# Prologue of a graph kernel: the first visit's tiles pass both convolutions ahead of the others, gather and copy back by visits

## The chip, the cores and the metric

The kernel runs on one core of one Trainium2 chip. The metric is the device time of one execution in microseconds; lower is better. Of the core's engines the text names TensorE (PE in the profile; PEld is its weight load), VectorE (DVE), ScalarE (ACT), GpSimd (POOL) and SyncE (SP), which here only issues DMAs. Each engine works through its own list of instructions in order; semaphores hold one engine until another has got somewhere.

## The reference

The input `x` is 64 graphs of 128 nodes with 128 features, `adj` 64 matrices of 128 x 128. Two stages follow each other, each with a residual and a layer norm over the features:

```
def gcn(x, adj):                          # on the first 25 nodes of each graph only
    for g, idx in enumerate(GROUPS):      # 25, 9, 7, 6, 6 nodes
        A = normalise(adj[:, idx][:, :, idx] + eye)
        h   = relu(A @ (x[:, idx] @ W1[g]) + b1[g])       # 128 -> 256
        out = relu(A @ (h @ W2[g]) + b2[g])               # 256 -> 128
        fused[:, idx] += softmax(fusion_w)[g] * out
x = layernorm(x + gcn(x, adj))
A = (adj != 0)
h = x
for l in range(5):
    h = gru(A^T @ (h @ weight[l]), h)     # one GRU cell, shared weights
out = layernorm(x + h * mask)
```

## The kernel before

All is written out by hand: five lists of instructions, one for each engine, with counters that one engine waits on and another raises. No planner orders anything; what stands first in the program of an engine runs first.

The 64 graphs are sixteen **visits** of four graphs each, and four **chunks** of sixteen graphs (four visits). The GRU layers run in 80 windows, four visits in turn; window k multiplies one visit's state by the gate weights (TensorE), applies the gates (ScalarE, VectorE) and forms the difference `dg` (GpSimd). The first stage of chunk c + 1 is spread over windows of chunk c. Only chunk 0 has nothing to hide behind: it is computed in the **prologue**, and this is what the change touches.

In the prologue the group of 25 nodes is four tiles (`TA`) of four graphs each, 100 rows; tile t is just visit t. The small groups are five tiles (`TB`): group 1 in two tiles of eight graphs, groups 2, 3 and 4 in one tile each of sixteen. For both halves the order is: adjacency transposed and scaled (`na`, `nb`), product with the node rows `xt` (`neighbours`, into `ya`, `yb`), W1 and ReLU (`hidden_a`, `hidden_b`), W2 (`second_a`, `second_b1`, `second_b2`, into `s2`), product with `na` or `nb` (`output_a`, `output_b`). ScalarE writes group 0 into `fused` and the small groups into `part`; VectorE adds `part` into `fused` with five adds (`gather`). Then TensorE multiplies the GRU's input weights for layers 2 to 4 (`fused_weights`), transposes `fused` back for all four visits (`back_visit`, waits for all five adds) and runs filler: 18 transposes of the identity (`stay_warm`) and 12 products with no reader.

For each visit VectorE adds the transposed rows into `xn` (`add_visit`) and takes the statistics (`norm1`); GpSimd makes the reciprocal root with a power (`deviation1`); the normalisation is shared, two graphs on ScalarE and two on GpSimd, for visit 0 on VectorE instead of GpSimd (`half_norm1`). Then TensorE transposes the visit into the GRU's layout (`enter`, lines 1247 and the waits ahead of it) and the windows begin. GpSimd also turns `an` into the 0/1 mask for visits 2 and 3 (`ones`), VectorE for visits 0 and 1. The lists that matter here, of VectorE and of GpSimd:

```
gather(0); ones(0); add_visit(0); norm1(0); add_visit(1); norm1(1)
half_norm1(0, HALVES[1]); add_visit(2); add_visit(3); lo_state(0, PL)
...
ones(2); deviation1(0); deviation1(1); norm1(1)
ones(3); deviation1(2); norm1(2); power(1)
```

Of the kernel before, what the change touches and what calls it, by code (L numbers as in the profile page):

```python
# [7 lines left out]
NG = len(GROUPS)  # L8
# [121 lines left out]
def build(nc, x, adj, nodemask, W1, b1, W2, b2, fusion_w, weight, w_ih, w_hh, b_ih, b_hh, out):  # L130
# [3 lines left out]
    with ctx:  # L134
# [5 lines left out]
        def sem(name):  # L140
# [77 lines left out]
        ALONE = dict(adj=(P[0], P[2]), y=(P[5], P[4]), ha=(P[0], P[2]), hb=(P[5], P[3]), s=(P[4], P[1], P[0]),  # L218
                     o=(P[2], P[5]))

# [6 lines left out]
        def b1c(g, c):  # L227
            return biasc[:, g * HC + c:g * HC + c + 1]
# [22 lines left out]
            "bn1", "ln1_st", "ln1_rs", "ln1_ok", "sum_ok", "bn2", "ln2_st", "ln2_rs", "ln2_ok", "out_ok"))  # L251
        gathered, dev1, dev2, ln1_dve, ln1_pool, hT_ok, ln2_dve = map(sem, (
# [64 lines left out]
        ADDS = 5  # L317

# [53 lines left out]
        def _(pool):  # L372
# [97 lines left out]
            ones(2)  # L470
# [3 lines left out]
            ones(3)  # L474
            deviation1(2)
            norm1(2)
            power(1)
# [35 lines left out]
        def _(act):  # L513
# [38 lines left out]
            def hidden_b1(c):  # L552

                act.wait_ge(h_ps, 4 * c + 4)
# [67 lines left out]
            neighbours(0)  # L622
# [107 lines left out]
        def _(dve):  # L730
# [75 lines left out]
            def neighbours(c):  # L806

                dve.wait_ge(y_ps, 2 * c + 2)
                nc.vector.tensor_copy(yb[:], banks(c)["y"][1][:, 0:COLS_B]).then_inc(yb_ok, 1)

            def hidden_b0(c):

                dve.wait_ge(h_ps, 4 * c + 3)
                for g in range(1, NG):
                    a, b = group_cols(g)
                    last = TS(hb[:, 0, a:b], banks(c)["hb"][0][:, a:b], b1c(g, 0), 0.0, ALU.add, ALU.max)
                last.then_inc(hb0_ok, 1)

            def second_b1(c):

                dve.wait_ge(s_ps, 3 * c + 2)
                nc.vector.tensor_copy(s2[0:ROWS[4], 4:6, :], banks(c)["s"][1][0:ROWS[4], 0:256].rearrange("p (t d) -> p t d", t=2)).then_inc(sb_ok, 1)

            def second_b2(c):

                dve.wait_ge(s_ps, 3 * c + 3)
# [4 lines left out]
            def gather(c):  # L831

                dve.wait_ge(oa_ok, c + 1)
                for g, done, (into, these) in gather_parts():
                    dve.wait_ge(ob_ok, (NG - 1) * c + g)
                    if done:
                        dve.wait_ge(gathered, ADDS * c + done)
                    TT(into, into, these, ALU.add).then_inc(gathered, 1)
# [213 lines left out]
        def _(pe):  # L1052
# [61 lines left out]

            def hidden_a(c):
# [87 lines left out]
            stay_warm(8, P[5])  # L1203
# [3 lines left out]
            TR(P[3][:, GATES:512], wl[:, 4, :], ident[:]).then_inc(prep_t, 1)  # L1207
            pe.wait_ge(wit_ok, 1)
# [9 lines left out]
            neighbours(0)  # L1218
# [3 lines left out]
            pe.wait_ge(w1_in, 16)  # L1222
            hidden_a(0)
            pe.wait_ge(prep_a, 1)
            hidden_b(0)
            pe.wait_ge(w2_in, 16)
            second_a(0)
            pe.wait_ge(prep_lo, 3)
            second_b1(0)
            second_b2(0)  # L1230
            output_a(0)
            output_b(0)
            pe.wait_ge(mask_in, 16)
            TR(P[3][:, GATES:GATES + B], maskr[:], ident[0:B, 0:B])
            fused_weights(2)
            fused_weights(3)
            fused_weights(4)
            pe.wait_ge(gathered, ADDS)
            for visit in range(SLOTS):
                back_visit(visit)  # L1240
            stay_warm(18, PG)
            for _ in range(12):
                MM(PG[:, 0:128], wh[:, 0, 0:128], wh[:, 0, 128:256], start=True, stop=True)
# [162 lines left out]
```

## Time and profile before

| | |
|---|---|
| median of 3 runs | 534.74 us (534.69 to 535.28) |
| the profiled execution | 534.39 us |
| its span, first to last instruction | 532.1 us |
| TensorE busy | 514.9 us (97%) |
| VectorE, ScalarE, GpSimd busy | 437.5, 369.4, 249.3 us |

A row of the timeline merges instructions of one line that follow each other; its first number is when the first starts, its second how long all of them take. Matmul ends are modelled and overlap the next start, so several matmuls in a row go out faster than their lengths add up to. An fp32 matmul is two matmul instructions ("passes"), a transpose one. The idle time in square brackets is that of the engine just before the row, with what ended it. Spans on GpSimd are rough.

### The profile page before, as it was taken

The numbers are of one execution on the slowest core, as the hardware profiler recorded it, in microseconds if no ns is written. First come the engines' busy times: TensorE is split into PE (matmuls) and PEld (weight loads), VectorE is DVE, ScalarE is ACT, GpSimd is POOL, SyncE is SP. The second block draws the span as 40 slices with busy tenths as digits, with TensorE's granted clock in tenths as the row PEclk, the third lists the DMA queues.
The fourth block names the chain that finished last, engine by engine and source line by source line (L and its number), as shares of the span: only waits on it lengthen the run. The fifth ranks groups of instructions, "written<-read, shape, count | busy, mean of one in ns | idle before, by whom it ended". The sixth has DMA issues, their size and how long they took to land.

```text
span 532.1 us, 8535 instructions
## 1 busy us (share of the span) xinstructions
PE 514.9 (97%) x2993; PEld 441.2 (83%) x2993; DVE 437.5 (82%) x970; ACT 369.4 (69%) x683; POOL 249.3 (47%) x299
## 2 busy tenths in 40 slices
PE   7999999999999999999999999999999999999991
PEld 6888889888888889888888889888888888888870
DVE  5479775899979877889979986688988998877886
ACT  2468665767876676787786676787785678786645
POOL 7569422458532354457633254546552245332334
PEclk9999999999999999999999999999999999999995
DMA  5967610000000000000000000000000000010002
GB/s 138 220 181 178 165 34 4 1 1 0 2 1 0 9 25 22 21 20 22 1 1 1 1 0 22 22 20 21 0 2 1 1 1 20 25 37 0 1 0 79
DMA packets 35579, 17.29 MB, mean 32 GB/s; under 512 B 4321, under 2 KB 35498, under 8 KB 35538
## 3 DMA queue, kind: packets, MB, share of 16 engines
q1 hardware_dynamic: 32233, 14.99, 10.7%
q10 hardware_dynamic: 2665, 1.54, 1.0%
q8 instruction: 24, 0.39, 0.3%
q0 software_dynamic: 640, 0.22, 0.3%
q14 instruction: 17, 0.14, 0.1%
HBM read 12.54 MB, written 4.19 MB: 31 GB/s over the span
## 4 chain that ended last, share of the span: by engine, by line
PE 92%; DVE 3%; SPq 2%; DMA 1%; ACT 1%; POOL 1%; issue 0%; DVEq 0%; POOLq 0%
PE p L1260 20%; PE p L1262 20%; PE p L1261 20%; PE p L1254 13%; PE p L1247 8%; PE p L1138 3%; PE p L1112 1%; PE p L1131 1%; PE p L1121 1%; DMA xt<-in_x_dram 1%; SPq L273 1%; PE p L1176 1%; SPq L268 1%; PE p L1168 1%; DVE st L930 0%; PE p L1063 0%
## 5 line engine op out<-in xcount | busy, mean ns | idle before, releaser
L486 POOL TENSOR_TENSOR dg<-hT,ng 128x512 f32<-128x512 f32 x80 | 126.1, 1576 | 255.7 <-ACT ng L706 255.6
L1260 PE MATMUL p<-ghi,wf 128*128 128x512 f32 x240 | 101.1, 421 | 0.0
L1260 PE MATMUL p<-hhi,wh 128*128 128x512 f32 x237 | 99.6, 420 | 0.0
L1262 PE MATMUL p<-ghi,wf 128*128 128x512 f32 x240 | 94.4, 393 | 0.0
L1261 PE MATMUL p<-glo,wf 128*128 128x512 f32 x240 | 93.6, 390 | 0.0
L1262 PE MATMUL p<-hhi,wh 128*128 128x512 f32 x237 | 93.1, 393 | 0.0
L1261 PE MATMUL p<-hlo,wh 128*128 128x512 f32 x237 | 92.5, 390 | 0.0
L1010 DVE SCALAR_TENSOR_TENSOR cg<-p,biasc,rg 128x512 f32<-128x512 f32 x80 | 59.9, 748 | 37.8 <-ACT rg L688 36.8
L688 ACT ACTIVATE rg<-p,gb 128x512 f32<-128x512 f32 x80 | 55.4, 692 | 34.8 <-PE p L1262 29.0
L706 ACT ACTIVATE ng<-cg,biasc 128x512 f32<-128x512 f32 x80 | 57.9, 724 | 23.1 <-DVE cg L1013 22.7
L1254 PEld LDWEIGHTS p<-an,nat 128*128 128x128 f32 x512 | 66.9, 191 | 5.1
L702 ACT ACTIVATE zg<-p,gb 128x512 f32<-128x512 f32 x80 | 55.1, 688 | 18.0 <-PE p L1262 17.8
L1254 PE MATMUL p<-an,nat 128*128 128x128 f32 x512 | 67.3, 274 | 0.0
L901 DVE TENSOR_TENSOR hlo<-hT,hhi 128x512 fp32r<-128x512 f32 x76 | 66.2, 871 | 0.8
L1013 DVE TENSOR_TENSOR cg<-cg,p 128x512 f32<-128x512 f32 x80 | 55.1, 688 | 8.7 <-DVE cg L1010 0.5
L907 DVE TENSOR_TENSOR glo<-p,ghi 128x512 fp32r<-128x512 f32 x80 | 55.1, 690 | 5.5 <-ACT ghi L653 5.5
L915 DVE TENSOR_TENSOR hT<-ng,dg 128x512 f32<-128x512 f32 x80 | 55.5, 694 | 2.8
L913 DVE TENSOR_TENSOR dg<-zg,dg 128x512 f32<-128x512 f32 x80 | 55.1, 689 | 0.0
L1247 PE MATMUL p<-ident,hT 128*128 128x128 f32 x320 | 49.1, 276 | 5.4 <-DVE hT L915 5.3
L1262 PEld LDWEIGHTS p<-ghi,wf 128*128 128x128 f32 x240 | 45.0, 188 | 10.4
L684 ACT COPY nat<-p 128x512 f32<-128x512 f32 x64 | 37.7, 589 | 22.6 <-PE p L1247 21.9
L1262 PEld LDWEIGHTS p<-hhi,wh 128*128 128x128 f32 x237 | 44.5, 188 | 9.9
(157 smaller groups left out, 846.9 us busy)
## 6 DMA issues: line engine op xcount, KB each, us to landing
xn<-in_x_dram SPq DMA_DIRECT2D x8, 512.0 KB, 4.8
an<-in_adj_dram SPq DMA_DIRECT2D x8, 512.0 KB, 7.4
out_dram<-xn SPq DMA_DIRECT2D x15, 256.0 KB, 2.3
xt<-in_x_dram SPq DMA_DIRECT2D x16, 50.0 KB
w<-in_L_gnn_W_dram ACTq DMA_DIRECT2D x1, 640.0 KB, 5.8
w<-in_L_gnn_W_dram SPq DMA_DIRECT2D x1, 640.0 KB, 4.4
zg<-in_L_gnn_weight_dram ACTq DMA_DIRECT2D x1, 320.0 KB, 3.9
xt<-in_x_dram SPq DMA_DIRECT2D x8, 36.0 KB
```

The source lines that it names most:

```text
L486: nc.gpsimd.tensor_tensor(dg[:, w.k % 2, :], hT[:, w.slot, :], ng[:, w.k % 2, :], ALU.subtract).then_inc(d_ok, 1)
L688: nc.scalar.activation(rg[:, p, :], PR[:], ACT.Sigmoid, bias=gb[:, 0:1]).then_inc(r_ok, 1)
L702: nc.scalar.activation(zg[:, p, :], PZ[:], ACT.Sigmoid, bias=gb[:, 1:2]).then_inc(z_ok, 1)
L706: nc.scalar.activation(ng[:, p, :], cg[:, p, :], ACT.Tanh, bias=bin_).then_inc(n_ok, 1)
L901: TT(hlo[:, m % SLOTS, :], hT[:, m % SLOTS, :] if source is None else source[:], hhi[:, m % SLOTS, :], ALU.subtract).then_inc(lo_ok, 1)
L915: TT(hT[:, s, :], ng[:, p, :], dg[:, p, :], ALU.add).then_inc(h_ok, 1)
L1010: STT(cg[:, p, :], PH[:], bhn, rg[:, p, :], ALU.add, ALU.mult).then_inc(t1_ok, 1)
L1247: last = TR(bank[:, q * 128:(q + 1) * 128], src(q), ident[:])
L1254: last = MM(bank[:, q * N:(q + 1) * N], src(q), an[:, b + q, :], start=True, stop=True)
L1260: MM(bank[:], w[:, 0, cols], xhi, start=start, stop=False)
L1261: MM(bank[:], w[:, 0, cols], xlo, start=False, stop=False)
L1262: return MM(bank[:], w[:, 1, cols], xhi, start=False, stop=stop)
```

## The change

Only the prologue of chunk 0 changes; no arithmetic is dropped.

- TensorE's `neighbours(0)` becomes `first_neighbours`: tile 0 of group 0, then the five small-group tiles, then tiles 1 to 3. `first_chunk` replaces the steps from `hidden_a` to `output_b`: tile 0 passes W1 first, then the small groups, then tiles 1 to 3 as one block of 300 columns; W2 and the output likewise, tile 0 ahead, tile 1 before the small groups' output, tiles 2 and 3 after it. Tile 0 has banks of its own (`TILE0`).
- ScalarE copies and activates tile 0 apart from tiles 1 to 3; the activation of the small groups' output is split by visits: four small ones for visit 0, five for the others. VectorE copies `s2` of tiles 1 to 3 (`s1_ok`), which ScalarE did before.
- The gather is split: five adds for visit 0, five for visit 1, five for visits 2 and 3 (`gather_visits`), on VectorE. `back_visit(0)` waits for the first five only; then the three `fused_weights`, then `back_visit(1)`, `(2)`, `(3)`.
- GpSimd's `ones(2)` moves behind the second visit's half, `ones(3)` behind the third's.
- Filler: 8 becomes 14 and 7 are added early on; 18 becomes 8 and 12 becomes 8 at the end.

```diff
@@ places of the banks
+        TILE0 = dict(y=P[6], h=P[7], s=P[6], o=P[7])
+        LATER = slice(ROWS[0], COLS_A)
@@ GpSimd
-            ones(2)
             deviation1(0)
             deviation1(1)
             norm1(1)
-            ones(3)
+            ones(2)
             deviation1(2)
             norm1(2)
+            ones(3)
             power(1)
@@ ScalarE, prologue
-            neighbours(0)
+            act.wait_ge(y0_ps, 1)
+            nc.scalar.copy(ya[:, 0:ROWS[0]], TILE0["y"][:, 0:ROWS[0]]).then_inc(ya0_ok, 1)
+            act.wait_ge(y_ps, 2)
+            nc.scalar.copy(ya[:, LATER], ALONE["y"][0][:, LATER]).then_inc(ya_ok, 1)
             ...
-            hidden_a(0)
+            act.wait_ge(h0_ps, 1)
+            for h in range(HC):
+                nc.scalar.activation(ha[:, h, 0:ROWS[0]], ..., bias=b1c(0, h)).then_inc(ha0_ok, 1)
             hidden_b1(0)
-            second_a(0)
+            for h in range(HC):
+                act.wait_ge(h_ps, 3 + h)
+                nc.scalar.activation(ha[:, h, LATER], ALONE["ha"][h][:, LATER], ACT.Relu, bias=b1c(0, h)).then_inc(ha_ok, 1)
+            act.wait_ge(s0_ps, 1)
+            nc.scalar.copy(s2[0:ROWS[0], 0, :], TILE0["s"][0:ROWS[0], 0:D]).then_inc(sa_ok, 1)
             act.wait_ge(b_ok, 1)
-            output_a(0)
-            output_b(0)
+            act.wait_ge(o0_ps, 1)
+            nc.scalar.activation(by_rows[:, 0, :, 0:FN], TILE0["o"][:, 0:ROWS[0]]...).then_inc(oa0_ok, 1)
+            act.wait_ge(o_ps, 1)
+            for g in range(1, NG):
+                first_part(g, 0, SB).then_inc(ob0_ok, 1)
+            first_part(1, SB, SB)
+            first_part(1, 2 * SB, 2 * SB).then_inc(ob_ok, 1)
+            for g in range(2, NG):
+                first_part(g, SB, 3 * SB).then_inc(ob_ok, 1)
+            act.wait_ge(o_ps, 2)
+            nc.scalar.activation(by_rows[:, 1:, :, 0:FN], ALONE["o"][0][:, LATER]...).then_inc(oa_ok, 1)
             high_weights(2)
@@ VectorE, prologue
             second_b1(0)
             second_b2(0)
-            gather(0)
+            dve.wait_ge(s_ps, 3)
+            nc.vector.tensor_copy(s2[0:ROWS[0], 1:4, :], ALONE["s"][0][0:ROWS[0], D:4 * D]...).then_inc(s1_ok, 1)
+            gather_visits(0, SB, oa0_ok, ob0_ok, visit0_ok)
             ones(0)
             add_visit(0)
             norm1(0)
+            gather_visits(SB, SB, oa_ok, ob_ok, visit1_ok)
+            gather_visits(2 * SB, 2 * SB, oa_ok, ob_ok, gathered)
             add_visit(1)
@@ TensorE, the new middle
+                second(0, TILE0["s"], 0).then_inc(s0_ps, 1)
+                pe.wait_ge(prep_lo, 3)
+                second_b1(0)
+                second_b2(0)
+                pe.wait_ge(sa_ok, 1)
+                MM(TILE0["o"][:, 0:ROWS[0]], s2[0:ROWS[0], 0, :], na[0:ROWS[0], 0:ROWS[0]],
+                   start=True, stop=True).then_inc(o0_ps, 1)
+                pe.wait_ge(ha_ok, HC)
+                second(1, ALONE["s"][0], D)
+                output_b(0)
+                second(2, ALONE["s"][0], 2 * D)
+                second(3, ALONE["s"][0], 3 * D).then_inc(s_ps, 1)
+                ...
+                pe.wait_ge(s1_ok, 1)
+                for t in TA[1:]:
+                    ...
+                last.then_inc(o_ps, 1)
```

TensorE from the end of the outputs to the first entering transposes (line 1247 before, 1364 after; `p4<-ident,fused` is the first visit's way back, `p6<-ng,cg` the fused weights of layer 2). Before:

```order
L1234 MATMUL p3<-ident,maskr 128x64
L1057 MATMUL p6<-ng,cg 128x384
L1057 MATMUL p0<-ng,cg 128x384
L1057 MATMUL p3<-ng,cg 128x384
L1195 MATMUL p4<-ident,fused 25x128 x4
L1195 MATMUL p1<-ident,fused 25x128 x4
L1195 MATMUL p7<-ident,fused 25x128 x4
L1195 MATMUL p2<-ident,fused 25x128 x4
L1189 MATMUL p5<-ident 128x128 x18
L1243 MATMUL p5<-wh 128x128 x12
L1247 MATMUL p6<-ident,xn 128x128 x4
```

And after:

```order
L1233 MATMUL p3<-ident,maskr 128x64
L1237 MATMUL p2<-na,s2 128x100 x3
L1320 MATMUL p4<-ident,fused 25x128 x4
L1120 MATMUL p6<-ng,cg 128x384
L1120 MATMUL p0<-ng,cg 128x384
L1120 MATMUL p3<-ng,cg 128x384
L1320 MATMUL p1<-ident,fused 25x128 x4
L1320 MATMUL p7<-ident,fused 25x128 x4
L1320 MATMUL p2<-ident,fused 25x128 x4
L1314 MATMUL p5<-ident 128x128 x8
L1360 MATMUL p5<-wh 128x128 x8
L1364 MATMUL p6<-ident,xn 128x128 x4
```

The first visit's transposes now stand ahead of the three weights, behind the output of tiles 1 to 3 (line 1237); the other visits' stand behind the weights.

VectorE from the first visit's add into `xn` to its half of the normalisation (line 895 before, 953 after). Before:

```order
L845 TENSOR_TENSOR xn<-xn,p4 25x512
L871 BN_STATS st1<-xn 128x6 x4
L875 BN_AGGR ag1<-st1 128x2 x4
L845 TENSOR_TENSOR xn<-xn,p1 25x512
L871 BN_STATS st1<-xn 128x6 x4
L875 BN_AGGR ag1<-st1 128x2 x4
L895 TENSOR_SCALAR xn<-xn,rs1,nm1 128x128 x2
```

And after, from the ten adds that follow the first visit's statistics:

```order
L896 TENSOR_TENSOR fused<-fused,part 128x4x9
L896 TENSOR_TENSOR fused<-fused,part 128x4x6
L896 TENSOR_TENSOR fused<-fused,part 128x4
L896 TENSOR_TENSOR fused<-fused,part 128x2x3x4 x2
L896 TENSOR_TENSOR fused<-fused,part 128x8x9
L896 TENSOR_TENSOR fused<-fused,part 128x8x6
L896 TENSOR_TENSOR fused<-fused,part 128x8
L896 TENSOR_TENSOR fused<-fused,part 128x2x3x8 x2
L903 TENSOR_TENSOR xn<-xn,p1 25x512
L929 BN_STATS st1<-xn 128x6 x4
L933 BN_AGGR ag1<-st1 128x2 x4
L953 TENSOR_SCALAR xn<-xn,rs1,nm1 128x128 x2
```

The ten adds of the other visits now stand between the first visit's statistics and the second visit's add.

GpSimd from the end of the second visit's power to the first difference `dg` (masks: `an<-an`, line 421 before, 449 after; line 388 and 416 is `power(1)`). Before:

```order
L448 TENSOR_TENSOR nm1<-nm1,rs1 128x4
L438 TENSOR_SCALAR xn<-xn,rs1,nm1 128x128 x2
L421 TENSOR_SCALAR an<-an 128x512
L443 TENSOR_SCALAR rs1<-ag1 128x4
L444 TENSOR_SCALAR nm1<-ag1 128x4
L446 TENSOR_TENSOR rs1<-rs1,minus_half 128x4
L448 TENSOR_TENSOR nm1<-nm1,rs1 128x4
L438 TENSOR_SCALAR xn<-xn,rs1,nm1 128x128 x2
L388 TENSOR_TENSOR dinv<-safe,minus_half 128x9
L486 TENSOR_TENSOR dg<-hT,ng 128x512
```

And after:

```order
L466 TENSOR_SCALAR xn<-xn,rs1,nm1 128x128 x2
L449 TENSOR_SCALAR an<-an 128x512
L471 TENSOR_SCALAR rs1<-ag1 128x4
L472 TENSOR_SCALAR nm1<-ag1 128x4
L474 TENSOR_TENSOR rs1<-rs1,minus_half 128x4
L476 TENSOR_TENSOR nm1<-nm1,rs1 128x4
L466 TENSOR_SCALAR xn<-xn,rs1,nm1 128x128 x2
L449 TENSOR_SCALAR an<-an 128x512
L416 TENSOR_TENSOR dinv<-safe,minus_half 128x9
L514 TENSOR_TENSOR dg<-hT,ng 128x512
```

The mask that stood ahead of the first power now stands in the place of the second one, and the second one behind the third visit's half, ahead of `power(1)`.

## Rows read from the trace of the kernel before

**Rows 1.** Busy time by stretch (us; x instructions; granted clock, DMA), 35 to 515.

```profile
35.00:515.00 480.00, 479.72 (x2757) 411.31 (x2755) 404.33 (x823) 346.73 (x630) 217.90 (x240) 1.00 0.08 22
```

**Rows 2.** Timeline, TensorE: start, length, engine, line, operation, out<-in, count, [idle before].

```profile
16.03 1.35 PE L1112 MATMUL p<-nb,xt 72*128 72x72 f32 x10 [0.36 <-DMA xt<-in_x_dram]
17.48 1.61 PE L1121 MATMUL p<-ya,w 128*128 128x400 f32 x4
27.02 2.20 PE L1057 MATMUL p<-ng,cg 128*128 128x384 f32 x6
29.06 1.91 PE L1195 MATMUL p<-ident,fused 128*25 128x128 f32 x16
30.81 2.13 PE L1189 MATMUL p<-ident 128*128 128x128 f32 x18
32.69 1.53 PE L1243 MATMUL p<-wh 128*128 128x128 f32 x12
34.63 0.63 PE L1247 MATMUL p<-ident,xn 128*128 128x128 f32 x4 [0.40 <-ACT xn L590]
```

**Rows 3.** Timeline, ScalarE (ACT) and VectorE (DVE), first visit's way to its normalisation.

```profile
17.58 0.18 ACT L624 COPY biasc<-p 128x21 f32<-128x21 f32 x1 [1.39 <-PE p L1221]
25.07 0.41 DVE L829 COPY s<-p 96x256 f32<-96x256 f32 x1
26.93 1.45 ACT L580 ACTIVATE part<-p,fb,fw 128x144 f32<-128x144 f32 x4 [0.44 <-PE p L1176]
27.50 1.31 DVE L838 TENSOR_TENSOR fused<-fused,part 128x144 f32<-128x144 f32 x5 [2.02 <-ACT part L580]
29.77 0.68 DVE L845 TENSOR_TENSOR xn<-xn,p 25x512 f32<-25x512 f32 x1 [0.63 <-PE p L1195]
31.68 0.64 DVE L845 TENSOR_TENSOR xn<-xn,p 25x512 f32<-25x512 f32 x1
33.26 0.38 DVE L875 BATCH_NORM_AGGREGATE ag<-st 128x2 f32<-128x6 f32 x4
33.65 0.88 ACT L590 ACTIVATE xn<-xn,nm,rs 128x128 f32<-128x128 f32 x2 [2.88 <-POOL nm L448]
33.65 0.63 DVE L895 TENSOR_SCALAR xn<-xn,rs,nm 128x128 f32<-128x128 f32 x2
```

**Rows 4.** Groups by shape (busy us, mean ns of one), VectorE's adds at line 838.

```profile
L838 DVE TENSOR_TENSOR fused<-fused,part 128x144 f32<-128x144 f32 x1 | 0.4, 424 | 2.0 <-ACT part L580 2.0
L838 DVE TENSOR_TENSOR fused<-fused,part 128x16 f32<-128x16 f32 x1 | 0.2, 180 | 0.0
```

**Rows 5.** Timeline, GpSimd (POOL), 29 to 49 us.

```profile
29.02 1.95 POOL L421 TENSOR_SCALAR an<-an 128x512 f32<-128x512 f32 x1 [7.84 <-DMA an<-in_adj_dram]
31.84 0.21 POOL L443 TENSOR_SCALAR rs<-ag 128x4 f32<-128x4 f32 x1 [0.87 <-DVE ag L875]
39.20 0.28 POOL L443 TENSOR_SCALAR rs<-ag 128x4 f32<-128x4 f32 x1 [0.83 <-DVE ag L875]
41.15 0.89 POOL L438 TENSOR_SCALAR xn<-xn,rs,nm 128x128 f32<-128x128 f32 x2
43.89 1.29 POOL L486 TENSOR_TENSOR dg<-hT,ng 128x512 f32<-128x512 f32 x1
47.11 1.31 POOL L438 TENSOR_SCALAR xn<-xn,rs,nm 128x128 f32<-128x128 f32 x2
```

**Rows 6.** Timeline, VectorE and TensorE, where the fourth visit enters.

```profile
47.31 0.78 DVE L913 TENSOR_TENSOR dg<-zg,dg 128x512 f32<-128x512 f32 x1
49.51 0.63 PE L1247 MATMUL p<-ident,xn 128*128 128x128 f32 x4
```

**Rows 7.** Timeline, GpSimd and VectorE at the same time, 39.7 to 40.8 us.

```profile
39.72 1.04 POOL L446 TENSOR_TENSOR rs<-rs,minus_half 128x4 f32<-128x4 f32 x1
39.97 0.39 DVE L763 TENSOR_TENSOR am<-ac,member 128x225 f32<-128x225 f32 x1
```

More of the change, by code:

```diff
@@ L317, in build, with graphs_of, visit_parts, these @@
         ADDS = 5
+        def graphs_of(g, b0, nb):
+            a, b = group_cols(g)
+            if g == 1:
+                t, k0 = divmod(b0, 8)
+                return slice(a + t * ROWS[4], a + (t + 1) * ROWS[4]), 8, slice(k0, k0 + nb)
+            return slice(a, b), CB, slice(b0, b0 + nb)
+        def visit_parts(b0, nb):
+            into = fused[:].rearrange("p (b n) -> p b n", n=NP)[:, b0:b0 + nb, :]
+            def these(g):
+                cols, k, some = graphs_of(g, b0, nb)
+                return part[:, cols].rearrange("p (n k) -> p k n", k=k)[:, some, :]
+            yield 1, 0, (into[:, :, 0:9], these(1))
+            yield 2, 0, (into[:, :, 9:15], these(2)[:, :, 1:7])
+            yield 2, 1, (into[:, :, 0:1], these(2)[:, :, 0:1])
+            for g in (3, 4):
+                v = GROUPS[g][0]
+                cols, k, some = graphs_of(g, b0, nb)
+                yield g, 2, (into[:, :, v:v + 12].rearrange("p k (s n) -> p s n k", s=2)[:, :, 0:3, :],
+                             part[:, cols].rearrange("p (s n k) -> p s n k", s=2, n=3)[:, :, :, some])
         @block.sync
@@ L829, in second_b2, with gather_visits @@
                 nc.vector.tensor_copy(s2[0:ROWS[7], 7:9, :], bank[0:ROWS[7], 128:384].rearrange("p (t d) -> p t d", t=2)).then_inc(sb_ok, 1)
[L831 to L835, printed above, removed]
+            def gather_visits(b0, nb, rows_ready, parts_ready, signal):
+                dve.wait_ge(rows_ready, 1)
+                for g, done, (into, these) in visit_parts(b0, nb):
+                    dve.wait_ge(parts_ready, g)
                     if done:
-                        dve.wait_ge(gathered, ADDS * c + done)
-                    TT(into, into, these, ALU.add).then_inc(gathered, 1)
+                        dve.wait_ge(signal, done)
+                    TT(into, into, these, ALU.add).then_inc(signal, 1)
             def add_visit(visit):
@@ L961, in _ @@
             second_b2(0)
-            gather(0)
+            dve.wait_ge(s_ps, 3)
+            nc.vector.tensor_copy(s2[0:ROWS[0], 1:4, :],
+                                  ALONE["s"][0][0:ROWS[0], D:4 * D].rearrange("p (t d) -> p t d", t=3)).then_inc(s1_ok, 1)
+            gather_visits(0, SB, oa0_ok, ob0_ok, visit0_ok)
             ones(0)
@@ L1113, in neighbours, with first_neighbours, one @@
                     last.then_inc(y_ps, 1)
+            def first_neighbours():
+                def one(bank, t, nn):
+                    r, o = ROWS[t], OFF[t]
+                    return MM(bank[:, o:o + r], xt[0:r, t, :], nn[0:r, o:o + r], start=True, stop=True)
+                pe.wait_ge(xta_in, 16 * n_runs(TA))
+                pe.wait_ge(na_ok, 1)
+                one(TILE0["y"], 0, na).then_inc(y0_ps, 1)
+                pe.wait_ge(xt_in, 16 * n_runs(XT_SP))
+                pe.wait_ge(xt_pool_in, 16 * n_runs(XT_POOL))
+                pe.wait_ge(prep_lo, 2)
+                for i, t in enumerate(TB):
+                    pe.wait_ge(nb_ok, i + 1)
+                    last = one(ALONE["y"][1], t, nb)
+                last.then_inc(y_ps, 1)
+                for t in TA[1:]:
+                    pe.wait_ge(na_ok, t + 1)
+                    last = one(ALONE["y"][0], t, na)
+                last.then_inc(y_ps, 1)
@@ new lines, in first_chunk, with second @@
+            def first_chunk():
+                pe.wait_ge(w1_in, 16)
+                pe.wait_ge(ya0_ok, 1)
+                for h in range(HC):
+                    last = MM(TILE0["h"][:, h * 128:h * 128 + ROWS[0]], w1[:, 0, h * 128:(h + 1) * 128], ya[:, 0:ROWS[0]],
+                              start=True, stop=True)
+                last.then_inc(h0_ps, 1)
+                pe.wait_ge(ya_ok, 1)
+                pe.wait_ge(prep_a, 1)
+                hidden_b(0)
+                for h in range(HC):
+                    MM(ALONE["ha"][h][:, LATER], w1[:, 0, h * 128:(h + 1) * 128], ya[:, LATER],
+                       start=True, stop=True).then_inc(h_ps, 1)
+                pe.wait_ge(w2_in, 16)
+                pe.wait_ge(ha0_ok, HC)
+                def second(t, bank, at):
+                    r, o = ROWS[t], OFF[t]
+                    for h in range(HC):
+                        last = MM(bank[0:r, at:at + D], ha[:, h, o:o + r], w2[:, 0, h, :], start=(h == 0), stop=(h == HC - 1))
+                    return last
+                second(0, TILE0["s"], 0).then_inc(s0_ps, 1)
[10 more added lines that the diff above has]
+                second(3, ALONE["s"][0], 3 * D).then_inc(s_ps, 1)
+                pe.wait_ge(mask_in, 16)
+                TR(P[3][:, GATES:GATES + B], maskr[:], ident[0:B, 0:B])
+                pe.wait_ge(s1_ok, 1)
+                for t in TA[1:]:
+                    r, o = ROWS[t], OFF[t]
+                    last = MM(ALONE["o"][0][:, o:o + r], s2[0:r, t, :], na[0:r, o:o + r], start=True, stop=True)
+                last.then_inc(o_ps, 1)
@@ L1202, in _ @@
             last.then_inc(prep_t, 1)
-            stay_warm(8, P[5])
+            stay_warm(14, P[5])
             pe.wait_ge(wl_in, 16)
@@ L1207, in _ @@
             TR(P[3][:, GATES:512], wl[:, 4, :], ident[:]).then_inc(prep_t, 1)
+            stay_warm(7, P[5])
             pe.wait_ge(wit_ok, 1)
@@ L1217, in _ @@
             last.then_inc(prep_t, 1)
-            neighbours(0)
+            first_neighbours()
             nr = NG * HC + NG + 6
@@ L1221, in _ @@
             TR(P[3][:, 128:128 + nr], rows[:], ident[0:nr, 0:nr]).then_inc(prep_t, 1)
[L1222 to L1237, printed above, removed]
+            first_chunk()
+            pe.wait_ge(visit0_ok, ADDS)
+            back_visit(0)
+            for l in (2, 3, 4):
+                fused_weights(l)
+            pe.wait_ge(visit1_ok, ADDS)
+            back_visit(1)
             pe.wait_ge(gathered, ADDS)
[L1239 to L1242, printed above, removed]
+            back_visit(2)
+            back_visit(3)
+            stay_warm(8, PG)
+            for _ in range(8):
                 MM(PG[:, 0:128], wh[:, 0, 0:128], wh[:, 0, 128:256], start=True, stop=True)
```

27 lines of the change are left out of this document (21 added, 6 removed).

## The prediction

> **What bounds the kernel now.** I read the busy times by stretch first. From 35 to 515 us TensorE is busy for 479.72 of 480.00 us [rows 1]. So nothing behind the prologue gives time back: a microsecond by which the prologue ends later or earlier is one in the result. The prologue itself is then read in order of time, TensorE's rows first. The last x rows land at 16.03; from there no row of TensorE has an idle time ahead of it until 34.63 [rows 2], but its work from 30.81 on (18 transposes of the identity, 12 products that nobody reads) is only filler until the first visit is normalised. What it really waits for is a chain over four engines: transposes of `fused` at 29.06, the add into `xn` on VectorE at 29.77, statistics, the power on GpSimd from 31.84, two halves of the normalisation at 33.65 on VectorE and ScalarE, and the entering transposes at 34.63 [rows 2, 3, 5]. The reader is to see that ScalarE idled 2.88 us before its half, and that VectorE came to its half with nothing to spare: between the first visit's statistics and that half stand the second visit's add, from 31.68, and its statistics, which end at 33.64; the half begins at 33.65 [rows 3].
>
> **Part 1: how much earlier is the first add?** The first tile's product with `xt` (two passes) goes out early as before, and then TensorE waits for the same landing, 16.03. From there, by passes (an fp32 matmul has two; ten in 16.03 to about 17.2 and sixteen transposes in 29.06 to 30.81 give 0.11 us each [rows 2]): small groups to 17.22; the six passes for the large group's tiles 1 to 3, which before lay ahead of the landing and were free, cost 0.67, to 17.89; the bias transpose 0.16; the first tile's W1 0.45, to 18.50. The second product must wait for `biasc`, which ScalarE copies in 0.18 [rows 3] behind the copy of the three later tiles: 18.70. Then 16 passes (1.80), four of 300 columns (0.25 each and 0.1 for the first, scaled from 400 columns [rows 2]), and 30 passes for the second weights and the first tile's output (3.28): 24.88. That support ends on TensorE at 24.4, and VectorE's two copies of it (0.41 for the second [rows 3], some 0.25 for what the first adds) end at 25.05: TensorE goes on at 25.11. Ten passes of output (1.19) and eight for tiles 2 and 3: 27.17, ending 27.33. The new wait: VectorE copies 384 columns (0.41 for 256 [rows 3], so 0.56), TensorE resumes at 27.99, six passes, 28.66. Queued behind that wait stand the first visit's four transposes: 28.66, ending 29.26, and the add starts at **29.36 against 29.77**. What moved off this path are the three fused-weight products, 2.04 us (27.02 to 29.06 [rows 2]); what came onto it are the 0.67, two split products and three waits of together 1.1.
>
> The first visit's adds don't set this. ScalarE's four small activations behind the small groups' output (26.47) take at most the 1.45 of the four large ones [rows 3], by their 24 to 36 columns about 1.0, to 27.6; VectorE is at its copy until 27.9, then five adds. An add of 16 elements takes 180 ns, one of 144 takes 424 [rows 4]: 150 ns and 1.9 ns an element, the next beginning some 0.09 before the end. Five of 4 to 36 elements give 0.67, to 28.52, under TensorE's six passes.
>
> **Part 2: what stands between the first statistics and the first half.** VectorE is free 1.91 after the first add's start (29.77 to 31.68 [rows 3]): 31.27. Before, the second add was next. Now ten adds come first: 0.58 for the second visit and 0.78 for the last two (8 to 72 elements), to 32.63. Their transposes for the second visit start when its adds end (31.94), so that its add starts at 32.70. From its start VectorE needed 1.9 until it was free for the first half (31.68 to some 33.6); now to 34.6. The half takes 0.63 [rows 3]: 35.2, and the entering transposes could start at 35.31. TensorE's own queue says nearly the same: last adds 32.72, eight transposes 0.87, eight filler transposes 0.87, eight filler products 0.92 (12 in 1.53 with the tail [rows 2]): 35.4. So **35.40 against 34.63: 0.77 later**, though the visit's sum was 0.4 earlier. GpSimd's power of the first visit (31.43 to 33.20) and ScalarE's half (33.24 to 34.1) are early and hide under this. The moved weights end on TensorE at 31.14, their six ScalarE copies and the mask at 32.5, ahead of 33.2: nothing. The added filler of the first 10 us lies in waits for a DMA and for ScalarE: nothing. Bounds: adds as dear as now (1.31 for five [rows 3]) give 1.26 more, 2.0 in all; adds for nothing leave VectorE ready for its half at 33.2, ScalarE's end at 34.1 decides, and the term is -0.4. I take the line through the two measured sizes.
>
> **Part 3: GpSimd's masks.** `ones(2)` ran in 29.02 to 30.97, where GpSimd waited anyway; now it follows the second visit's half, and `ones(3)`, the same instruction, moves behind the third's [rows 5]. The second statistics come at 34.66, so power (1.8, as 31.84 to 33.65) and half (0.9) end at 37.47 and `ones(2)` at 39.39; the third statistics are due at 39.98 (39.20 shifted by 0.77), so this one is hidden. `ones(3)` has no such gap: behind it stand `power(1)`, the first difference `dg` and the fourth visit's power and half. All come 0.77 + 1.95 = 2.72 later: the half that ended at 48.42 ends at 51.14 [rows 5]. TensorE's entering transposes of the fourth visit, at 49.51, would be due at 50.28 [rows 6]; they start at 51.24, a wait of 0.96. ScalarE's half of it needs only the power and is ready before GpSimd's. VectorE's use of `dg` at 47.31 [rows 6], due at 48.08, finds it ready at 47.90. Bounds: the fourth visit's half took 1.31 where the same two instructions for the third took 0.89 [rows 5]; at 0.89 the wait is 0.54; if the first `dg`, 1.29, is stretched in its new neighbourhood by as much as that half was, 0.42, it is 1.4. I take **0.85**.
>
> **Sum.** The profiled execution took 534.39 for a span of 532.1. 0.77 + 0.85 = 1.6 makes 536.0 of it; the median of the three runs, 534.74, lies 0.35 above it, so the forecast is 536.3.
>
> **Rivals.**
> *The masks stay hidden* (not slower). Place: GpSimd between 42 and 51 us. It decides if GpSimd's row from the third half to the fourth runs 0.96 shorter than I add up, for instance because a power overlaps what is queued behind it. Then only part 2 is left: 534.74 + 0.77 = 535.5. For it speaks that spans on GpSimd are rough; against it that no row of GpSimd after the third statistics has an idle time ahead of it [rows 5].
> *The lead survives* (faster). Place: VectorE from 31.3 to 33.2. If the ten adds and the second visit's work fit there, the first half starts with ScalarE's, and the entering transposes at 34.2; with the masks hidden as well it is 534.74 - 0.4 = 534.3, with the masks late 535.2. Against it: the second add and its statistics alone are 1.9 of the 1.93 that lie there.
> *The adds are held up* (slower still). Ten adds with both inputs in SBUF now run while GpSimd takes the power of the first visit (31.88 to 32.92). If the power holds them, visits 1 to 3 are gathered some 0.9 later: 537.2. The trace has one such meeting: VectorE's `am<-ac,member` at 39.97, both inputs in SBUF, took 0.39 inside a power of 1.04 us that had begun 0.25 before [rows 7]; it wasn't held. The Trainium skill ("SBUF — State Buffer", section "Who interferes with whom") says that a VectorE instruction with two SBUF inputs and a GpSimd instruction that reads SBUF exclude each other for the whole instruction, the second blocking fully. By that rule this rival would be the forecast, 537.2; the row speaks against it here.
> *No lead at all*: if the three new waits in part 1 are each 0.15 longer, the first add is no earlier than 29.8 and everything is 0.45 later: 536.8.
>
> **How the numbers follow.** Forecast 536.3 with 0.60; held adds 0.08; no lead 0.07; masks hidden (or late masks with a surviving lead) 0.17; lead with hidden masks 0.08. About 0.2%, 1.07 us, is what a measurement of this kernel can tell from no change. Of the forecast's own spread (terms 0.4 to 1.2 and 0.55 to 1.4) a twentieth lies below 1.07. So slower 0.70, same 0.21, faster 0.09. The range goes from 534.7, which takes in the hidden masks and leaves out the surviving lead, to 537.4, which takes in the held adds and the dearer end of part 2.
>
> **What would show it.** Part 1: the add of the first visit starts at 29.1 to 29.6 and TensorE waits ahead of the output of the large group's tiles 1 to 3. Part 2: ten short adds stand between the first statistics and the second add, the first half on VectorE begins at 34.3 to 34.9, over a microsecond after ScalarE's, and TensorE's entering transposes at 35.2 to 35.7. Part 3: a GpSimd mask at 42.8 and TensorE idle for 0.5 us or more before the fourth visit's entering transposes, at 50.8 to 51.6. I am wrong if VectorE's first half starts with ScalarE's (part 2), or if TensorE enters the fourth visit without a wait (part 3).

## The result, and the profile after

The changed kernel takes 535.74 us (median of 20 executions, 535.18 to 539.62) against 534.75 for the kernel before in the same comparison (20 executions, 533.96 to 536.34): a ratio of 1.0036, 95% interval 1.002 to 1.0052. It is slower, by 1.0 us where 1.6 was forecast, and inside the range. But no execution lay near the forecast 536.3: twelve took 535.18 to 535.79, eight 537.23 to 539.62. The profiled one (535.2 us, span 532.9) is one of the twelve. The part behind the prologue has lost a microsecond of TensorE's work, 478.70 for 479.72 [rows 1]:

```profile
35.00:515.00 480.00, 478.70 (x2753) 410.70 (x2752) 403.36 (x822) 345.79 (x629) 219.53 (x240) 1.00 0.08 22
```

The timeline of TensorE, for [rows 2] and [rows 6] (start, length, engine, line, operation, out<-in, count, [idle before]):

```profile
14.66 0.44 PE L1182 MATMUL p<-na,xt 100*128 100x100 f32 x2
15.14 1.35 PE L1182 MATMUL p<-nb,xt 72*128 72x72 f32 x10
16.33 0.84 PE L1182 MATMUL p<-na,xt 100*128 100x100 f32 x6
...
27.09 0.91 PE L1237 MATMUL p<-na,s 100*128 100x100 f32 x6 [0.45 <-DVE s L1021]
27.84 0.60 PE L1320 MATMUL p<-ident,fused 128*25 128x128 f32 x4
28.27 2.10 PE L1120 MATMUL p<-ng,cg 128*128 128x384 f32 x6
31.23 0.62 PE L1320 MATMUL p<-ident,fused 128*25 128x128 f32 x4 [0.85 <-DVE fused L896]
...
34.69 0.62 PE L1364 MATMUL p<-ident,xn 128*128 128x128 f32 x4
...
50.74 0.63 PE L1364 MATMUL p<-ident,xn 128*128 128x128 f32 x4 [1.22 <-POOL xn L466]
```

The ten passes that need the last x rows start at 15.14, where they started at 16.03 in [rows 2]: in this execution the rows came earlier, and TensorE had nothing to wait for. All of the first part is therefore 0.9 early, and the first add is 1.2 early (28.55 for the 29.77 of [rows 3]). Still the first visit enters at 34.69, not earlier than the 34.63 of [rows 2]. The fourth visit enters behind a wait of 1.22 us, where [rows 6] had none. VectorE's timeline, for [rows 3], says where the 1.2 went:

```profile
28.55 0.68 DVE L903 TENSOR_TENSOR xn<-xn,p 25x512 f32<-25x512 f32 x1 [0.53 <-PE p L1320]
29.26 0.87 DVE L929 BATCH_NORM_STATS2 st<-xn 128x6 f32<-128x128 f32 x4
30.16 0.38 DVE L933 BATCH_NORM_AGGREGATE ag<-st 128x2 f32<-128x6 f32 x4
30.46 1.56 DVE L896 TENSOR_TENSOR fused<-fused,part 128x36 f32<-128x36 f32 x10
31.95 0.68 DVE L903 TENSOR_TENSOR xn<-xn,p 25x512 f32<-25x512 f32 x1
...
33.87 0.57 DVE L953 TENSOR_SCALAR xn<-xn,rs,nm 128x128 f32<-128x128 f32 x2
```

Ten adds stand between the first statistics and the second add. From the first add to VectorE's half it is 5.32 us (28.55 to 33.87) where it was 3.88 [rows 3], and ScalarE had started its half at 32.55. GpSimd's timeline shows the other part, for [rows 5]:

```profile
31.08 1.16 POOL L474 TENSOR_TENSOR rs<-rs,minus_half 128x4 f32<-128x4 f32 x1
...
36.72 1.95 POOL L449 TENSOR_SCALAR an<-an 128x512 f32<-128x512 f32 x1
...
42.04 1.94 POOL L449 TENSOR_SCALAR an<-an 128x512 f32<-128x512 f32 x1
43.96 1.82 POOL L416 TENSOR_TENSOR dinv<-safe,minus_half 128x9 f32<-128x9 f32 x1
45.76 1.27 POOL L514 TENSOR_TENSOR dg<-hT,ng 128x512 f32<-128x512 f32 x1
47.12 0.19 POOL L471 TENSOR_SCALAR rs<-ag 128x4 f32<-128x4 f32 x1
47.40 0.73 POOL L472 TENSOR_SCALAR nm<-ag 128x4 f32<-128x4 f32 x1
48.09 1.00 POOL L474 TENSOR_TENSOR rs<-rs,minus_half 128x4 f32<-128x4 f32 x1
49.17 0.20 POOL L476 TENSOR_TENSOR nm<-nm,rs 128x4 f32<-128x4 f32 x1
49.48 1.12 POOL L466 TENSOR_SCALAR xn<-xn,rs,nm 128x128 f32<-128x128 f32 x2
```

The fourth visit's mask at 42.04 has no idle time behind it until the half at 49.48: one row pushes the next, as forecast.

### The profile page after: what moved, and what is told of

Its sections match the earlier page's. It is cut to its first block, busy times and chain, and to the rows that moved or that the text cites. A ratio compares the mean times of both kernels' runs of the same rounds, so it can differ in the third digit from the quotient of the medians.

```text
span 532.9 us, 8569 instructions
## 1 busy us (share of the span) xinstructions
PE 516.2 (97%) x2996; PEld 442.0 (83%) x2996; DVE 438.9 (82%) x981; ACT 370.5 (70%) x692; POOL 249.1 (47%) x299
## 4 chain that ended last, share of the span: by engine, by line
PE 92%; DVE 4%; POOL 2%; ACT 1%; issue 1%; POOLq 0%; DVEq 0%
PE p L1377 20%; PE p L1379 20%; PE p L1378 20%; PE p L1371 13%; PE p L1364 8%; PE p L1263 3%; PE p L1314 2%; PE p L1256 1%; PE p L1175 1%; PE p L1301 1%; PE p L1246 1%; PE p L1126 1%; POOL rs L474 1%; PE p L1293 0%; PE p L1182 0%
```

## The experiments

The forecast's two losses can be read above. What it does not explain is the eight executions at 537 to 540. Twelve runs followed, in groups of the first four, the next four, then two and two; those of one group share a chip and the executions of the kernel before (medians there 534.41, 534.65, 534.43 and 534.52).

**The kernel as it is, again.** No edit.

> The changed kernel once more, unaltered, as the reference for the other runs on this chip. Theory (late masks on GpSimd cost the time): TensorE again waits 1.0 to 1.3 us ahead of the fourth visit's entering transposes, the time is 1 to 2 us above the kernel before. Second theory, for the runs near 539 us that show a lower mean clock (0.984 to 0.986 against 0.989 to 0.991): some executions lose the clock for a few us after TensorE's new waits near 27 and 31 us; then about 4 of 10 executions lie 2 to 4 us above the others, and a profile of one shows a stretch granted 0.5 behind 27 us. Rival: these runs come from the landing of the x rows, and move by no more than the 0.9 us by which the two profiles differ there (16.03 against 15.14).

Measured: 535.38 (12 executions; ten at 535.12 to 536.25, two at 539.1), ratio 1.0027 (1.0009 to 1.0045). The profiled execution shows the same two losses, a wait of 1.22 ahead of the fourth visit among them; the x rows landed early again.

**Masks put back.**

```
@@ GpSimd
+ones(2)
 deviation1(0)
 deviation1(1)
 norm1(1)
-ones(2)
+ones(3)
 deviation1(2)
 norm1(2)
-ones(3)
 power(1)
```

> Only GpSimd's two masks return to where they stood before (ones(2) ahead of the first power, ones(3) behind the second visit's half). Theory of the late masks: TensorE's wait of 1.22 us ahead of the fourth visit's entering transposes goes, and the time falls by 1.0 to 1.3 us against the unaltered changed kernel, to that of the kernel before within 0.3. The first power may start up to 0.4 later, which ScalarE's half and VectorE's later half hide. Rival (the wait has another cause, or VectorE's queue ahead of the first half costs the time): within 0.3 us of the unaltered changed kernel.

Measured: 536.47, ratio 1.0032 (1.0009 to 1.0055), but the median hides two groups: five executions at 533.99 to 534.30, seven at 536.27 to 539.76. The lower group is 1.1 us under the lowest of the kernel as it is (535.12), and the profile shows no wait above 0.1 us ahead of the fourth visit. So the late masks cost 1.1 us, where the forecast had charged them with 0.85. The profiled execution fell in the upper group (537.97), and shows what that is. TensorE's timeline and the stretches behind it (busy us by engine PE, PEld, DVE, ACT, POOL; then TensorE's granted clock, DMA share, GB/s):

```profile
14.69 0.44 PE L1182 MATMUL p<-na,xt 100*128 100x100 f32 x2
15.93 2.01 PE L1182 MATMUL p<-nb,xt 72*128 72x72 f32 x10 [0.81 <-DMA xt<-in_x_dram]
```

```profile
15.00:16.00 1.00, 0.19 (x3) 0.07 (x1) 0.46 (x3) 0.40 (x3) 1.00 (x2) 1.00 0.54 106
16.00:17.00 1.00, 1.00 (x7) 1.00 (x8) 0.00 (x0) 0.00 (x0) 1.00 (x3) 0.72 0.95 273
17.00:18.00 1.00, 1.00 (x7) 1.00 (x6) 0.03 (x1) 0.00 (x0) 1.00 (x3) 0.50 1.08 298
...
22.00:23.00 1.00, 1.00 (x6) 1.00 (x6) 0.66 (x3) 0.00 (x0) 0.33 (x1) 0.50 0.96 252
23.00:24.00 1.00, 1.00 (x8) 0.94 (x7) 0.90 (x6) 0.21 (x1) 0.00 (x0) 0.86 1.13 302
24.00:25.00 1.00, 1.00 (x8) 0.79 (x7) 0.20 (x2) 1.00 (x5) 0.00 (x0) 1.00 1.19 299
```

Between tile 0's product and the late x rows TensorE stands idle for 0.81 us; then the granted clock reads 0.50 (1.2 GHz) from 16.4 to 23.3. The same ten passes take 2.01 us instead of 1.35.

**The later waits filled.** Transposes that nobody reads, ahead of the waits at 27, 31 and 32 us.

```
+stay_warm(4, P[6])
 pe.wait_ge(s1_ok, 1)
...
+stay_warm(7, P[1])
 pe.wait_ge(visit1_ok, ADDS)
 back_visit(1)
+stay_warm(2, P[7])
 pe.wait_ge(gathered, ADDS)
```

> 13 transposes of the identity are put into TensorE's three new waits (4 ahead of the output of tiles 1 to 3, 7 ahead of the second visit's transposes, 2 ahead of the third's), nothing else. Theory of the clock: the executions 2 to 4 us above the others go, the fast ones stay where they are within 0.2 us. Rival (landing, or anything not on TensorE): the upper group stays, about 4 of 10.

Measured: 538.14, ratio 1.0067 (1.0044 to 1.0089). The three waits are gone from the timeline, the upper group isn't: nine of twelve executions lie over 1.5 us above the lowest (two of them, 537.14 and 537.32, by time outside of the span, 4.1 and 4.2 us where 2.2 is usual). The profiled execution (541.10) waited 1.06 us for the x rows and then ran at a granted clock of 0.50 from 16.1 to 26.3:

```profile
16.04 2.22 PE L1182 MATMUL p<-nb,xt 72*128 72x72 f32 x9 [1.06 <-DMA xt<-in_x_dram]
```

```profile
16.00:26.00 10.00, 9.96 (x41) 9.25 (x42) 3.24 (x13) 2.81 (x10) 5.15 (x8) 0.50 1.05 247
```

So it isn't the waits that the change adds later that lower the clock here. The profile of the changed kernel says the same: its waits of 0.85 us at 31.23 and of 1.22 us at 50.74 are as long, and its clock reads 1.00 from 13 to 62 us.

**VectorE's half ahead of the second add.**

```
 gather_visits(2 * SB, 2 * SB, oa_ok, ob_ok, gathered)
+half_norm1(0, HALVES[1])
 add_visit(1)
 norm1(1)
-half_norm1(0, HALVES[1])
...
-stay_warm(8, PG)
-for _ in range(8):
+stay_warm(3, PG)
+for _ in range(0):
```

> VectorE's half of the first visit's normalisation moves ahead of the second visit's add and statistics, and TensorE's filler at the end is cut from 8 transposes and 8 products to 3 transposes, so that it does not stand in the way. Theory of the order (the half stands behind too much): TensorE's entering transposes begin 1.0 us earlier and the time falls by about as much. Rival (VectorE's whole queue is the bound: the adds of visits 2 and 3 must be done before the first window's products anyway, and they end no earlier): the entering transposes are earlier by 1.0, the first window's products by only 0.3, and the time falls by at most 0.4.

Measured: 536.54, ratio 1.0067 (1.0042 to 1.0092), lowest 536.1. The first visit enters 4.99 us after the first add (34.13 to 39.12; 6.14 in the kernel as it is), but the first window's products don't gain from it:

```profile
39.12 0.63 PE L1364 MATMUL p<-ident,xn 128*128 128x128 f32 x4
39.59 1.06 PE L1371 MATMUL p<-an,xn 128*128 128x128 f32 x8
41.95 0.47 PE L1410 MATMUL p<-hhi,wh 128*128 128x512 f32 x1 [1.31 <-DVE xn L903]
```

They wait for VectorE's adds of visits 2 and 3, and start 7.82 after the first add where it was 7.43 (28.55 to 35.98). VectorE itself stood 0.54 us still ahead of the half, whose scale GpSimd had not finished. In this order the entry of the first visit isn't the bound; VectorE's whole queue up to the rows of the fourth visit is. Neither time that was expected came: the lowest execution is 1.0 us above the lowest of the kernel as it is. The first products are 0.4 later against the first add, and from them to the fourth visit's entry it is 15.44 us (41.95 to 57.39) where it was 14.76; what lengthens that stretch is not shown.

**The six passes put back.** Tiles 1 to 3 of the first group stand again ahead of the wait for the x rows; the two semaphore counts follow.

```
 one(TILE0["y"], 0, na).then_inc(y0_ps, 1)
+for t in TA[1:]:
+    pe.wait_ge(na_ok, t + 1)
+    last = one(ALONE["y"][0], t, na)
+last.then_inc(y_ps, 1)
 pe.wait_ge(xt_in, 16 * n_runs(XT_SP))
...
-for t in TA[1:]:
-    pe.wait_ge(na_ok, t + 1)
-    last = one(ALONE["y"][0], t, na)
-last.then_inc(y_ps, 1)
```

> The changed kernel with one thing put back: the six passes of tiles 1 to 3 of the first group stand again between tile 0's product and the wait for the last x rows. Theory: the executions at 537 to 539 us come from TensorE idling 0.8 us or more at 15.1 to 16.2 us when the x rows land late, after which the granted clock reads 0.5 for 7 to 10 us. With six passes (0.67 us) in that place the idle is 0.4 us or less, as in the kernel before, the granted clock stays 1.0 from 13 to 27 us, and the executions above 536.5 become as rare as in the kernel before (3 of 34), with a median of 535.0 to 535.6. The wait ahead of the fourth visit stays 1.2 us. Rival (the drop comes from the new waits at 27 to 32 us or from anything else in the new order): about a third of the executions stay above 536.5 us.

Measured: 535.19 (ten of eleven at 534.86 to 535.75, one at 537.67), ratio 1.001 (0.9995 to 1.0024). The wait ahead of the fourth visit is still 1.22. Of the kernel before, two of the 34 executions in the first group lie above 536.5, not three. In the profiled execution the rows landed late, and the clock held (1.00 in each stretch from 13 to 36 us):

```profile
14.50 1.11 PE L1182 MATMUL p<-na,xt 100*128 100x100 f32 x8
16.06 1.35 PE L1182 MATMUL p<-nb,xt 72*128 72x72 f32 x10 [0.45 <-DMA xt<-in_x_dram]
```

**Filler in their place.** The order of the change, with six idle transposes in that spot.

```
+stay_warm(6, P[7])
 pe.wait_ge(xt_in, 16 * n_runs(XT_SP))
```

> The changed kernel in its own order, with six idle transposes (0.11 us each, 0.67 us) between tile 0's product and the wait for the last x rows. Theory: the idle there is what lowers the clock, so filling it with passes that do no work takes the executions above 536.5 us away as well; the six passes then cost up to 0.67 us where the rows land early and nothing where they land late, so the median is 535.3 to 536.0 with a narrow spread. Rival (the order of the tiles matters, not the idle): a third of the executions stay above 536.5 us and the others come out up to 0.67 us later.

Measured: 536.04, ratio 1.003 (1.0009 to 1.0051); ten of eleven at 535.41 to 536.43, one at 541.42. The profile shows 0.37 us of idle and a clock of 1.00 from 13 to 36 us:

```profile
15.84 1.35 PE L1182 MATMUL p<-nb,xt 72*128 72x72 f32 x10 [0.37 <-DMA xt<-in_x_dram]
```

So what counts is the idle time, not which passes fill it; and useful passes there are worth 0.85 us in the median over idle ones.

**Both put back.** The edits of the second and the fifth run together; the ten adds and the copy back by visits stay.

> Both undone: tiles 1 to 3 of the first group again ahead of the wait for the x rows, and the masks of visits 2 and 3 again at their old places in GpSimd's order. The ten adds and the copy back by visits stay as changed. Theory (the idle before the x rows and the late masks are all that the change loses in the end): fourth visit entered without a wait above 0.2 us, no executions above 536.5 beyond the 3 of 34 of the kernel before, median 534.0 to 534.6, that is no measurable difference to the kernel before. Rival (the adds on VectorE's path cost about 1 us to the end by themselves): median 535.0 or more.

Measured: 534.37, ratio 1.0001 (0.9984 to 1.0019): the change's loss is gone. No wait of 0.15 us or more ahead of the fourth visit. From the six passes put back to this run the lowest time falls by 1.06 (534.86 to 533.80), the price of the late masks again. Four of twelve executions still lay at 536.15 to 537.63, at mean granted clocks of 0.984 to 0.987, against the theory: with the six passes in place such executions are rarer over all runs, but not gone.

**Three graphs on ScalarE, one on VectorE.** As the last, and:

```
-norm1(0, HALVES[0])
+norm1(0, range(SB - 1))
...
-half_norm1(0, HALVES[1])
+half_norm1(0, range(SB - 1, SB))
```

> As the kernel with the tiles ahead and the masks put back, and of the first visit's four graphs ScalarE normalises three and VectorE one, where it was two and two: one scaling (0.32 us, started every 0.23 us) leaves VectorE's queue behind the second visit's statistics, and ScalarE had waited 0.92 us there for the scale. Theory (VectorE's queue from the first add to the fourth visit's rows is what times the first window): the first visit is entered 0.2 us earlier, and the median is 0.1 to 0.3 us under that kernel, 533.8 to 534.4. Rival (the GRU's start is timed by something else, so that the wait only moves on): within 0.1 us of it.

Measured: 534.29, ratio 0.9994 (0.9979 to 1.0009), two of twelve at 536.3 to 536.7. VectorE's half ends at 34.19, but the first visit enters 6.16 after the first add, as good as the 6.14 of the changed kernel: TensorE was still in its filler, without an idle time.

**Four more idle transposes ahead of the x rows,** and the three-one kernel again, on one chip.

```
+stay_warm(4, P[7])
 pe.wait_ge(xt_in, 16 * n_runs(XT_SP))
```

> As the kernel with tiles ahead, masks put back and three graphs on ScalarE, with four idle transposes (0.44 us) more ahead of the wait for the last x rows. Before, 2 of 12 executions of that kernel, and 4 of 12 of the one without the last step, still came 2 us above the fastest. Theory (those come from what is left of the idle ahead of the x rows, up to 0.45 us): none or one of 12 does here, with a median of 534.0 to 534.6. Rival (they come from another idle time, or from nothing in the prologue's order): two or more of 12 still do.

> The same kernel without the four transposes, that is the three-one kernel again, to be counted beside it on the same chip: median 533.9 to 534.5, two or three of 12 executions 2 us above the fastest.

Measured: 534.30 (534.08 to 534.64), ratio 0.9998 (0.9989 to 1.0007), and 534.15 (533.65 to 534.46), ratio 0.9989 (0.9978 to 0.9999). Neither had an execution above 534.7, so the count tells nothing about the four transposes.

**Less filler ahead of the entry.**

```
-stay_warm(8, PG)
-for _ in range(8):
+stay_warm(6, PG)
+for _ in range(6):
```

> As the three-one kernel, with the filler ahead of the first visit's entry cut from 8 transposes and 8 products to 6 and 6. In that kernel VectorE's share of the first normalisation ended at 34.19 us and the entering transposes started at 34.72, right behind the filler, without an idle time. Theory (TensorE's own queue of filler is what holds the entry there): the filler ends 0.44 us earlier, the first visit is entered 0.35 to 0.45 us earlier, at some 5.75 us after the first add's start where it was 6.16, and the median is 0.3 to 0.4 us under the three-one kernel's 534.15 to 534.29, so 533.7 to 534.0 and measurably under the kernel before. Rival (the first window's products wait for VectorE's adds of visits 2 and 3, as they did in the run with the half ahead of the second add): a wait of 0.3 us or more at the first window's products takes it back, 534.1 to 534.4.

Measured: 534.23, ratio 0.9989 (0.9976 to 1.0002). The mechanism is there: the first visit enters 5.79 after the first add (31.18 to 36.97), the first products come 7.09 after it instead of 7.46, and they don't wait. So here, with one scaling less in VectorE's queue, an earlier entry does reach the first products. The time isn't: 0.37 us in one place can't be told from the spread of 0.9 us among the eleven ordinary executions. The profiled execution was the twelfth (536.60), and suggests what the four at 536 to 538 above may be. The x rows landed later still, and even behind the six passes TensorE idled:

```profile
14.29 1.11 PE L1182 MATMUL p<-na,xt 100*128 100x100 f32 x8
16.64 1.35 PE L1182 MATMUL p<-nb,xt 72*128 72x72 f32 x10 [1.24 <-DMA xt<-in_x_dram]
```

```profile
17.00:18.00 1.00, 1.00 (x10) 0.91 (x9) 0.00 (x0) 0.00 (x0) 1.00 (x3) 1.00 0.84 184
18.00:19.00 1.00, 0.97 (x6) 0.80 (x7) 0.84 (x2) 0.68 (x3) 1.00 (x2) 0.89 0.72 76
19.00:20.00 1.00, 1.00 (x6) 1.00 (x6) 0.67 (x3) 0.46 (x2) 0.92 (x3) 0.50 1.07 302
...
22.00:23.00 1.00, 1.00 (x6) 0.88 (x6) 0.64 (x5) 0.49 (x2) 0.00 (x0) 0.91 1.12 302
```

**All four graphs on ScalarE.** As the last, with `norm1(0)` for `norm1(0, range(SB - 1))`, no half on VectorE, TensorE's wait for that half gone, and five products of filler.

> As the run with less filler, ScalarE normalises all four graphs of the first visit, VectorE none, and one product less of filler. Theory: VectorE's queue gives another 0.23 us, ScalarE needs 0.39 us more and ends at some 34.1, so the entry is 0.0 to 0.1 us earlier and the median is within 0.1 us of the run with less filler. Rival (VectorE's adds of visits 2 and 3 time the first window): 0.2 us under it.

Measured: 534.41, ratio 0.9995 (0.9984 to 1.0006). It tells neither theory: TensorE waited 0.56 us for ScalarE, since GpSimd's mask, put back ahead of the first visit's power, started only at 29.27 when the adjacency rows had landed, ended at 31.22 and held the power until 31.81. That is a price of the old place of the masks, seen in this profile: where the adjacency comes late, the first visit's scale does too.

## Why the prediction came out as it did

*Part 1 was right, against its own landing.* From the ten passes to the first add it forecast 13.33 us (16.03 to 29.36); it took 13.41 (15.14 to 28.55), and 13.74 before. TensorE waits ahead of the output of tiles 1 to 3, as forecast, 0.45 us for the 0.66 of the working.

*Part 2 was right.* From the first add to the entry: forecast 6.04, measured 6.14, before 4.86. The ten adds took 1.49 to the start of the next, where 1.36 was reckoned from [rows 4]; VectorE's half at 33.87 is 1.3 us behind ScalarE's. TensorE's own filler ends only as the entry begins, 0.25 behind VectorE's half (34.44): the forecast had the two as close (35.4 and 35.31). Against the landing, the entry is 0.95 later (19.55 for 18.60), where 0.77 was forecast.

*Part 3 had the right mechanism and a term too small,* 1.22 for 0.85. The working came to 0.96 and was taken down to 0.85, for the case that the half of the fourth visit is shorter than the 1.31 it was charged with. It was, 1.12; but GpSimd's second short row, `nm`, took 0.73 at 47.40 (0.71 in the kernel as it is, again) where the run with the masks put back has 0.20. VectorE's `dg` product ran at the same time (47.38 to 48.07); whether that stretched it isn't shown. The forecast had looked for a stretched row in the half and in `dg`, and it was in neither. That the wait goes with the masks' places, and with it 1.1 us of the lowest time, was shown by the second run, and again by the fifth and the seventh.

*The sum, made against one landing, is short of what was measured:* 0.95 and 1.22 are 2.2 us. Yet the median moved by 1.0, and here is the step that failed. "The six passes for the large group's tiles 1 to 3, which before lay ahead of the landing and were free, cost 0.67": that step took the landing at 16.03 as fixed, and the idle time left ahead of it as free. Neither holds. In ten of the fourteen profiled executions here TensorE waited for the rows, and the ten passes start between 15.22 and 16.64; in that of the changed kernel they start at 15.14 without a wait. Where the rows land early, the kernel before can't use it, since the six passes fill the time up to about 15.7 (with three graphs on ScalarE the ten passes follow the six at 15.64 without an idle time); the changed kernel can, and the profiled execution got 0.9 back: 2.2 - 0.9 = 1.3, of which the span, with a quicker last write, shows 0.8. Where they land late, the changed kernel's order idles for 0.8 us and more; the three profiles of it that do (second to fourth run) then read a clock of 0.50 for 6.8 to 10.2 us. Even the landing of the forecast, 16.03, would leave an idle time of that size (it was 0.81 at 15.93). The changed kernel's own eight slower executions lie 2 to 4 us above the twelve. The forecast lies between the two cases, where no execution was; that the median came out inside the range is in part luck, since it rests on twelve of the twenty executions being of the faster kind.

How far this is shown: of the runs without passes or filler in that place 30 of 67 executions took over 1.5 us more than the lowest of the same run (28 if the two with their extra time outside of the span are left out); of those with them 10 of 92; of the kernel before 10 of 132 (one execution of 1345 us aside). Filling this idle made such executions rarer, filling the others didn't, and each of the four profiles with a clock of 0.50 has 0.8 us or more of idle there. It is the idle time and not the late landing itself: with the six passes ahead the clock held where the ten passes started at 16.06 (the six passes put back) and at 16.11 (three graphs on ScalarE, again); without them it fell where they started at 15.93 and 16.04. The runs with passes or filler used other chips than those without; the kernel before, which ran beside all of them, has 1 of 20, 3 of 34, 2 of 35, 1 of 21 and 3 of 22 such executions, so the chip is an unlikely cause, but the changed kernel itself was not run beside them. What stays open: no execution of the changed kernel's own upper group was profiled, and of its eight, three show a mean granted clock of 0.989, as the twelve do; only the other five, at 0.984 to 0.986, show a lower one.

*The rivals.* Held adds: false. The adds of visits 1 to 3 ran at 0.17 to 0.29 us each, from 30.46 to 32.02, and five of them inside GpSimd's power of 31.08 to 32.24. The Trainium skill ("SBUF — State Buffer", section "Who interferes with whom") has the two exclude each other; the trace doesn't agree, and shows at most the power at 1.16 for 1.04. Masks hidden: false in every profile of the changed order (1.22 to 1.27 us). The lead that survives: false, ScalarE waits for VectorE. No lead: false, 0.33 us are there. The rival that was missing was an idle TensorE, here ahead of the x rows, behind which the clock falls.

## What to carry to other kernels

Work that stands ahead of a wait for a transfer can cost twice when it is moved behind it: its own time, and, where the transfer is late, half the clock for a stretch behind the idle time that it leaves (3.4 to 10.2 us in the four profiles here). Ask of every such wait how far the landing varies from run to run, not only when it was in the profile; a kernel whose executions fall into two groups has a median that describes neither. And a stage that hands its first result over early gains little while one engine's queue, here VectorE's up to the fourth visit's rows, must be through before the next stage can run on: an entry 1.15 us earlier brought the first products nothing, and one 0.37 earlier came through where that queue had been shortened. With both losses put back the new order of the copy back was worth nothing measurable against the kernel before, and the best of the repaired versions, three graphs on ScalarE (0.9994 and 0.9989 in two runs) and less filler (0.9989), are no better than a measurement of this kernel can tell.

## What the runs showed of the hardware

The granted clock fell to 0.50 after one idle time of TensorE of 0.81 us (masks put back), though TensorE had been at work, in good part with filler, in the microseconds before. It read 0.50 for 6.8 us there, and for 10.2 us with the later waits filled and with the half first, while TensorE was busy again throughout; in the last of these it fell at 15.7, still within the idle time. With six passes ahead and 1.24 us of idle it read 1.00 for 2.1 us more, fell at 18.8 and came back at 22.2. In the ten profiles with 0.54 us of idle or less there it read 1.00 from 13 to 36 us. The length of one idle time doesn't decide by itself: behind waits of 0.85 us (31.23) and 1.22 us (50.74) in the changed kernel, and of 1.31 us (41.95) with the half first, it stayed at 1.00. What else decides is not shown by these runs. In the ten profiles in which TensorE waited for the last x rows, it went on at 15.22 to 16.64 us, though the programs are nearly the same.
